# Score products of a quantised attention: 32 rows in place of 128, and two kinds of them in turn

## The reference

```
q = _fq_sym(q, axis=-1); k = _fq_sym(k, axis=-1); v = _fq_sym(v, axis=2)
attn = jnp.einsum('bhqd,bhkd->bhqk', q, k)
attn = jax.nn.softmax(attn.astype(jnp.float32), axis=-1)
attn = _fq_unsigned(attn, axis=-1)
out = jnp.einsum('bhqk,bhkd->bhqd', attn, v)
```

## Time and profile before

| | us |
|---|---|
| median of 3 runs | 688.63 (687.92 to 689.13) |
| profiled execution, its span | 687.7 |
| TensorE busy | 651.0 (95%) |
| VectorE busy | 576.4 (84%) |
| ScalarE busy | 417.5 (61%) |
| GpSimd busy | 389.1 (57%) |
| line 1843, 512 products, busy | 140.4 |
| line 1892, 256 maxima, busy | 159.6 |
| line 1885, 128 exponentials, busy | 153.5 |

### The profile page before, as it was taken

How to read it: one execution, slowest core, us unless ns; L and a number is a source line. 1 busy time by engine, 2 the same in 40 slices (tenths; PEclk the granted TensorE clock), 3 DMA queues, 4 the chain that set the end, 5 groups by cost and what they waited for, 6 DMA issues and landing times.

```text
span 687.7 us, 13890 instructions
## 1 busy us (share of the span) xinstructions
PE 651.0 (95%) x5088; PEld 410.1 (60%) x5088; DVE 576.4 (84%) x1029; ACT 417.5 (61%) x697; POOL 389.1 (57%) x500
## 2 busy tenths in 40 slices
PE   8899999999999999999999999999889889988887
PEld 6456766666666676766766666654436444544453
DVE  5998987887897797899989769888877889999655
ACT  5644454444544465565654445549878899899941
POOL 5876666566557736689965516526635543345401
PEclk9999999999999999999999999999989999999999
DMA  9666689765756588988974965639998899999900
GB/s 309 164 147 140 146 184 172 173 140 122 158 122 151 120 196 215 210 173 193 184 168 118 226 144 115 148 81 218 235 186 153 168 149 198 160 185 163 201 14 9
DMA packets 347827, 111.01 MB, mean 161 GB/s; under 512 B 313704, under 2 KB 344432, under 8 KB 347760
## 3 DMA queue, kind: packets, MB, share of 16 engines
q1 hardware_dynamic: 347760, 110.13, 77.1%
HBM read 31.97 MB, written 0.26 MB: 47 GB/s over the span
## 4 chain that ended last, share of the span: by engine, by line
PE 67%; DVE 21%; ACT 5%; issue 3%; DMA 2%; POOL 1%; DVEq 0%; ACTq 0%; POOLq 0%
PE psum L1060 21%; PE psum L1032 20%; DVE tops L1892 8%; PE psum L1843 6%; PE psum L1046 5%; PE psum L506 3%; ACT cT L1885 3%; DVE neg_max L1272 2%; PE psum L1908 2%; DMA c_nat<-cT 2%; PE psum L1085 1%; PE psum L1095 1%; PE psum L827 1%; PE psum L845 1%; DVE e_lo L1260 1%
## 5 line engine op out<-in xcount | busy, mean ns | idle before, releaser
L1060 PE MATMUL psum<-c_nat,eT 128*128 128x256 f16 x1536 | 188.1, 273 | 0.9 <-ACT u_sb L1234 0.9
L1892 DVE TENSOR_REDUCE tops<-psum 128x1 f32<-128x512 f32 x256 | 159.6, 683 | 20.7 <-PE psum L1843 20.1
L1885 ACT ACTIVATE cT<-psum,bias,q_scale 128x1024 f16<-128x1024 f32 x128 | 153.5, 1204 | 22.6 <-PE psum L1843 21.1
L1032 PE MATMUL psum<-cT,qk 128*128 128x512 f16 x744 | 165.6, 379 | 0.1
L1060 PEld LDWEIGHTS psum<-c_nat,eT 128*128 128x128 f16 x1536 | 147.3, 98 | 24.1 <-issue 1.6
L1843 PE MATMUL psum<-kT,v_space 128*128 128x512 f16 x512 | 140.4, 389 | 9.4 <-DVE tops L1892 7.3
L1032 PEld LDWEIGHTS psum<-cT,qk 128*128 128x128 f16 x744 | 72.6, 98 | 82.3 <-issue 1.2
L1272 DVE TENSOR_REDUCE neg_max<-psum 128x1 f32<-128x2048 f32 x32 | 73.2, 2287 | 21.3 <-PE psum L1032 21.2
L1260 DVE TENSOR_TENSOR e_lo<-e_all,e_hi 128x2048 f16<-128x2048 f32 x32 | 88.5, 2767 | 0.0
L1843 PEld LDWEIGHTS psum<-kT,v_space 128*128 128x128 f16 x512 | 45.4, 99 | 71.4 <-DVE tops L1892 34.4
L1203 ACT ACTIVATE e_all<-psum,neg_max 128x2048 f32<-128x2048 f32 x32 | 63.1, 1970 | 16.5 <-DVE neg_max L1274 16.4
(11 more groups left out here) (286 smaller groups left out, 947.3 us busy)
## 6 DMA issues: line engine op xcount, KB each, us to landing
wvo_h<-in_L_xattn_Wv SPq DMA_DIRECT2D x30, 128.0 KB, 2.4
wvo_h<-in_L_xattn_Wo SPq DMA_DIRECT2D x30, 128.0 KB, 2.3
wqk_h<-in_L_xattn_Wq SPq DMA_DIRECT2D x28, 128.0 KB, 2.4
wqk_h<-in_wkT SPq DMA_DIRECT2D x28, 128.0 KB, 2.6
mx_land<-in_mx_weights SPq DMA_DIRECT2D x8, 384.0 KB, 4.0
v_space<-in_ctx SPq DMA_DIRECT2D x4, 512.0 KB, 5.8
cT<-in_ctx SPq DMA_DIRECT2D x2, 1024.0 KB, 8.3
c_nat<-in_expert_wT SPq DMA_DIRECT2D x2, 1024.0 KB, 6.6
```

The source lines that it names most:

```text
L1032: ins = pe.matmul(s_ps[:, n * 512:(n + 1) * 512], c.qk[:, u % 2, q_part, k, :], m.cT[:, b, c_part, 4 * n:4 * n + 4, k, :], start=(k, q_par ...
L1060: ins = pe.matmul(u_ps, c.eT[:, v % 2, e_part, j, :], m.c_nat[:, v // H0, c_part, j, :], start=(j, e_part, c_part) == (0, 0, 0), stop=(j, ...
L1885: act.activation(m.y[:, u % 2, q * CHUNK:(q + 1) * CHUNK], m.bank(second_place(u, q), 2), ACT.Exp, bias=m.bias[:, u:u + 1], scale=m.q_scal ...
L1892: dve.tensor_reduce(m.tops[:, n // NB, n % NB:n % NB + 1], m.bank(n % 3), AX.X, ALU.max, negate=True).then_inc(s["q_max"], 1)
```

## The change

`pe_scores` takes the 32 rows of the head in place of all 128, in both uses; the zeros are no longer read. In `pe_attention` the first of a chunk's two first products now stands between its two second ones, and the other behind them. Which products are made, their columns, their banks and all waits are as before; each wait moves with its product.

```diff
-def pe_scores(pe, m, u, ps, at):
+def pe_scores(pe, m, u, ps, at, own_rows):
     b, group, r = u // H1, u % H1 // KG, u % KG
-    return pe.matmul(ps, m.qT[:, b, group, r, :], m.kT[:, group, at:at + BLK], start=True, stop=True)
+    rows = slice(r * DW, (r + 1) * DW) if own_rows else slice(0, P)
+    return pe.matmul(ps, m.qT[rows, b, group, r, :], m.kT[rows, group, at:at + BLK], start=True, stop=True)
...
-    pe_scores(pe, m, n // NB, m.bank(n % 3), n % NB * BLK).then_inc(s["q_first"], 1)
+    pe_scores(pe, m, n // NB, m.bank(n % 3), n % NB * BLK, True).then_inc(s["q_first"], 1)
...
-def pe_second(pe, m, s, u, q):
+def pe_second(pe, m, s, u, q, between=()):
...
-        ins = pe_scores(pe, m, u, m.bank(second_place(u, q) + k), q * CHUNK + k * BLK)
+        ins = pe_scores(pe, m, u, m.bank(second_place(u, q) + k), q * CHUNK + k * BLK, True)
+        for n in between[k:k + 1]:
+            pe_first(pe, m, s, n)
     ins.then_inc(s["q_second"], 1)
...
         for q in range(NC):
+            due = range(AHEAD + NB * u + 2 * q, min(AHEAD + NB * u + 2 * q + 2, NB * UNITS))
             if u < UNITS:
-                pe_second(pe, m, s, u, q)
-            for n in range(AHEAD + NB * u + 2 * q, AHEAD + NB * u + 2 * q + 2):
-                if n < NB * UNITS:
-                    pe_first(pe, m, s, n)
+                pe_second(pe, m, s, u, q, due[0:1])
+                due = due[1:]
+            for n in due:
+                pe_first(pe, m, s, n)
```

## The result

| | before | after |
|---|---|---|
| median | 688.3 us | 718.7 us |
| runs | 687.7 to 689.1 | 713.9, 714.1, 723.3, 723.4 |
| profiled execution, its span | 687.7 us | 712.6 us |
| mean granted clock of TensorE over it | 0.993 | 0.861 |

The ratio is 1.0438, with a 95% interval of 1.0373 to 1.0503: the kernel is slower by 4%, where 0.6% faster was forecast, and the time lies far above the range. A ratio leaves out a run that is over 1.5% above the fastest of its kernel; that is one run here, of units_9_12 (700.1 us).

The account below looks back on a forecast made before the run. Bounds by stage: TensorE's order to 466 us, DMA to 503, TensorE to 562, VectorE to 649. Terms 1.5 - 5.2 - 0.5 = -4.2 us gave 684.4 us from 688.6; range 679 to 693 us.

Parts of the forecast that it names:

- The pair's step: Two score products of different heads: 0.22 us if they go together, 0.43 us one behind the other; 0.22 taken.
- The switch: Each change between products of few rows and of 128 rows costs 0.1 us, bounds 0 and 0.2; 201 switches counted.
- moved wait: First score's wait for VectorE's bank read, now ahead of the exponentials' second half: 0 taken, 0 to 1.5 us.
- The first stage's +1.5 us: 442 to 466 us: nearly nothing pairs, 21 switches cost 2.1 us, partly in waits: +1.5 us, 0 to +3.
- 503 to 562 us: TensorE is the bound and gets about 9.7 us free; ScalarE is late next: -5.2 us, from -7.5 to -2.
- about 35: Whole kernel: TensorE gives back about 35 us of its work, four fifths of it not on the path.
- the clock: Rival, chance 0.15: TensorE does less, half clock for half of 503 to 562 us; changes cancel to 0, 688.6 us.
- 562 to 649 us: VectorE is the bound and can take only its 0.6 us of waiting: -0.5 us, -2 to +1.5.
- The stretch from 466 to 503 us: DMA engines full and SyncE's queue unbroken, so TensorE's gain buys nothing: 0, at most -1.6 us.
- no overlap: Rival, chance 0.17: pairs go one behind the other, only switches are left: +8 us, 696.6 us.

Follow-up runs that it names:

- units_9_12: 32 rows and the new order only in the slots of units 9 to 12, all else as before the change: 689.5 us, 1.0039.
- turn_only: The changed kernel's new order, but with all 128 rows as before: 691.0 us, 1.0031.
- one_group: The changed kernel with every score product on the 32 rows of the group's first head, other heads' scores left out: 802.5 us, 1.1654.
- late_units: 32 rows and the new order only from unit 16 on (562 us), all ahead as before the change: 704.1 us, 1.0223.
- fill2: The changed kernel with 128 rows kept in `pe_cross` and two unread 128-row products ahead of each chunk from unit 1 on: 725.0 us, 1.0528.
- fill1: The changed kernel with one unread 128-row product ahead of each chunk from unit 1 on: 739.6 us, 1.0726.
- rows_only: The changed kernel's 32 rows, but with the order of before (second, second, first, first): 721.5 us, 1.0471.

## Why the prediction was wrong

**What held.** The pair's step, taken at its lower bound of 0.22 us, is 0.22 us. The switch, taken as 0.1 us from line 1712's rows, is worked out from the starts in the changed kernel at whole clock: a value product behind a score begins 0.307 us after it in place of 0.215, a score behind a value product 0.101 in place of 0.025, a score behind an fp32 product 0.311 in place of 0.216, and an fp32 product behind a score 0.402 in place of 0.216 (the usual distances where nothing is waited for, from 4 to 8 places each): 0.08 to 0.19 us each. The new order with its moved wait costs what turn_only shows, 2.3 us, more than the bound of 1.5 that I gave the wait. It does not hold VectorE up: in turn_only, from 570 to 640 us, VectorE waits 0.3 us for scores, as before. The first stage's +1.5 us came as +1.3. That is no proof of its switches: the clock was at half behind 464.0 us, and has a part in it. And while the clock was whole the kernel did gain in 503 to 562 us, but less than forecast: the ten slots of units 9 to 12 at whole clock make 6.27 us a unit, and the same slots before 6.56. That is 0.3 us a unit (0.3 in units_9_12 too), by estimate some 2.6 us for the nine units of this stage in place of 5.2. A slip besides: the terms of the sum give TensorE 32 us back behind 466 us (49.7 less 17.4), not about 35.

**The step that failed** is that the sum leaves the clock whole: every stage's term takes what TensorE gives back off the path to cost nothing, and half clock stands only as the rival "the clock", with a chance of 0.15 and a price that leaves the time where it was. Three things in that rival were wrong.

Its condition: I argued against it that both falls before had come behind waits, that a pair leaves only short gaps, and that the clock had stayed whole from 562 to 649 us. one_group shows that gaps are not what it hangs on: the clock is halved with TensorE busy throughout, when its products read 32 rows. And the third argument was drawn from products of 128 rows; late_units, which changes this stretch alone, has it at half.

Its extent: I took half clock for half of the time from 503 to 562 us; it was at half for 198 of the 218 us from 464 to 682.

Its price: I took +1.5 us for 562 to 649 us, with no sum for it, where 14.9 us were lost; a unit takes 6.80 us in place of 5.81. Set slot by slot against the kernel before, about half of this lies in the 30 slots with value products. At half clock such a chunk takes TensorE 1.50 us against ScalarE's 1.2, so ScalarE waits at each of them: units 16 and 18, which have no side products, take 5.40 us in place of 4.85. The larger part, 10.4 of the 14.9 us, lies in the 24 slots, ten of them with value products too, in which TensorE also runs side products (two of unit 20's went from 2.21 to 3.40 us and from 2.11 to 3.05). What I had doubled was not all doubled: a value product of 16 columns begins 0.027 us behind the one before in place of 0.025, while a product of 512 columns does so 0.427 us behind in place of 0.216.

The stretch from 466 to 503 us, where I gave 0 because SyncE's queue was the bound, lost 5.5 us. At half clock TensorE is busy 40.6 of 42.5 us there, ScalarE's wait for scores went from 1.6 to 4.7 us, and SyncE's queue, unbroken before, now waits for exponentials. In order of time:

```profile
479.62 1.02 SPq L1450 DMA_DIRECT2D expert_wT<-in_expert_wT  x1
481.26 7.57 SPq L1984 DMA_TRANSPOSE c_nat<-cT  x2
```

The first row ends at 480.64, 0.6 us ahead of the next, and of the two transposes the first ended at 484.57 and the second began at 486.86, when its exponentials were done.

**The rival "no overlap"** was the one with the large price, and it did not come; that its 696.6 us lay nearest to the measured time is chance.

**What stays open.** Where turn_only's 2.3 us go. Why the clock fell three times in fill2 (at 540.6, 564.5 and 622.5 us), though each chunk had two products of 128 rows added. Why the changed kernel's runs fall into two sets, 714 and 723 us: their mean clocks were 0.861 and 0.846, so the clock fits, but only one of the two was profiled. And whether filling the array at a place off ScalarE's path would have kept the clock without cost; it was not tried.

The Trainium skill's rule that tiles of different rows run in parallel (TensorEngine Tiling, Key Properties) holds in this trace, with 0.004 us between the starts.

## What to carry to other kernels

Work that TensorE does not need may still be what keeps its clock up. Before products are cut to fewer rows or packed side by side, look at the stages in which TensorE waits for others: there the saving buys nothing, and if the clock falls to half, its long products there take double (0.427 us in place of 0.216). Look at the granted clock of each stage first, ahead of any busy time, and cost such a change at both clock levels, slot by slot, not as a mean over a stage.

## What the runs showed of the hardware

- Two score products on different 32 rows and different banks start 0.004 us apart, and the next pair follows 0.22 us later, which is the step of a single product; on the same rows they start 0.216 us apart (0.427 at half clock).
- With score products of 32 rows TensorE's clock was granted at half (1.2 GHz) while TensorE was busy 80.00 of 80.00 us (one_group). With 128 rows in the same order it was whole but for 3.4 us (turn_only, behind 442 us).
- Once down, the clock stayed down: 140 us on end in the changed kernel and 307 us in one_group, until the products of 128 rows of the kernel's tail. It rose between where expert products stand (at 484.5 and 525.4 us in the changed kernel). With 64 rows, or with products of 128 rows added (fill1, fill2), it rose more often.
- Score products did not always start in the program's order: in rows_only, written second, second, first, first, a first product on other rows started 0.007 us behind the chunk's first one and ahead of its second, which needs the same rows as that one, in 101 of 112 chunks.
- At half clock products of 512 columns start 0.427 us apart in place of 0.216, products of 16 columns 0.027 in place of 0.025.
- A switch between products of 32 and 128 rows costs 0.08 to 0.19 us at whole clock and 0.08 to 0.14 us between scores and value products at half (0.562 in place of 0.426, 0.107 in place of 0.027).
